# Three empty 32-byte pieces in the on-chip memory map of a decoder layer

## The reference

```python
x = x + attention(layernorm(x))        # 32 query heads, 8 key/value heads of 128; keys and values:
                                       # 16 cache blocks of 32 tokens picked by block_idx, and the 128 new ones
x = x + cross_attention(layernorm(x), ctx_4096, mask)   # 32 heads of 128, rmsnorm with ln_weight, position bias
x = x + (gelu(layernorm(x) @ W1 + b1) @ W2 + b2)        # 512 -> 2048 -> 512, NaN in y set to 0
```

## Time and profile before

| | |
|---|---|
| median of 3 runs | 2126.07 us (2125.66 to 2126.80) |
| the profiled execution's own time | 2129.9 us |
| its span, first to last instruction | 2128.0 us |
| TensorE matmul busy (PE) | 2076.8 us, 98% |
| TensorE weight load busy (PEld, beside PE) | 1789.8 us, 84% |
| VectorE busy (DVE) | 1500.9 us, 71% |
| ScalarE busy (ACT) | 1017.3 us, 48% |
| GpSimd busy (POOL) | 548.7 us, 26% |
| granted TensorE clock, mean | 0.991 of full speed |
| DMA | 76.90 MB, mean 36 GB/s; busy in the first 45 us |

### The profile page before, as it was taken

The page is one execution under the profiler, slowest core; times in us unless marked ns, Lnnn a source line. Parts: engine busy times, 40 slices in busy tenths (PEclk is TensorE's granted clock), DMA queues, the critical chain, the costliest instruction groups (busy, mean ns, idle before and its releaser), DMA issues.

```text
span 2128.0 us, 33928 instructions
## 1 busy us (share of the span) xinstructions
PE 2076.8 (98%) x11620; PEld 1789.8 (84%) x11620; DVE 1500.9 (71%) x2365; ACT 1017.3 (48%) x2232; POOL 548.7 (26%) x428
## 2 busy tenths in 40 slices
PE   8999999999999999999899999999999999999996
PEld 7888888888888888888788888888888888877885
DVE  6777777777777777777766666666666666677776
ACT  3555555555555555555544444444444444433331
POOL 2222122212221222221222222222222222214223
PEclk9999999999999999999999999999999999999998
DMA  8000000000000000011011111111111111010111
GB/s 234 16 21 16 15 20 20 16 14 20 20 20 10 20 20 20 13 47 40 31 59 43 42 42 37 38 39 38 42 42 42 42 42 42 23 35 25 49 44 50
DMA packets 44162, 76.90 MB, mean 36 GB/s; under 512 B 7378, under 2 KB 13650, under 8 KB 43602
## 3 DMA queue, kind: packets, MB, share of 16 engines
q1 hardware_dynamic: 43826, 74.15, 11.6%
q10 hardware_dynamic: 288, 2.10, 0.3%
HBM read 74.13 MB, written 2.10 MB: 36 GB/s over the span
## 4 chain that ended last, share of the span: by engine, by line
PE 88%; DVE 6%; issue 3%; ACT 2%; DMA 1%; SPq 0%; DVEq 0%; ACTq 0%
PE bank L1087 22%; PE bank L1089 22%; PE bank L1088 22%; PE bank L1156 9%; PE bank L1202 6%; PE bank L1355 1%; PE bank L1354 1%; PE bank L1270 1%; PE bank L1271 1%; PE bank L1329 1%; DVE negmax L872 1%; DVE V_lo L866 1%; DVE xn L802 1%; DVE pT_lo L910 1%; DVE q_lo L904 1%
## 5 line engine op out<-in xcount | busy, mean ns | idle before, releaser
L882 DVE SCALAR_TENSOR_TENSOR xacc<-bank,rinv,xacc 128x512 f32<-128x512 f32 x512 | 375.7, 745 | 71.2 <-PE bank L1089 71.1
L481 ACT ACTIVATE pT_hi<-bank 128x512 fp32r<-128x512 f32 x320 | 190.8, 597 | 202.3 <-PE bank L1202 202.0
L872 DVE TENSOR_REDUCE negmax<-bank 128x1 f32<-128x640 f32 x256 | 210.2, 821 | 36.9 <-PE bank L1156 29.6
L535 ACT ACTIVATE prob<-bank,negmax 128x640 f32<-128x640 f32 x256 | 202.6, 791 | 66.2 <-DVE negmax L872 66.2
L910 DVE TENSOR_TENSOR pT_lo<-bank,pT_hi 128x512 fp32r<-128x512 f32 x320 | 217.5, 680 | 2.4 <-ACT pT_hi L481 2.4
L1202 PE MATMUL bank<-ident,prob 128*128 128x128 f32 x1280 | 191.3, 272 | 0.0
L1202 PEld LDWEIGHTS bank<-ident,prob 128*128 128x128 f32 x1280 | 159.2, 140 | 18.6
L378 POOL TENSOR_TENSOR wo_lo<-wo_raw,wo_hi 128x512 fp32r<-128x512 f32 x32 | 41.4, 1293 | 430.8 <-ACT wo_hi L481 430.8
L628 ACT ACTIVATE xprob<-xscore,negmax 128x128 f32<-128x128 f32 x256 | 99.5, 391 | 96.2 <-DVE negmax L963 96.2
L1087 PE MATMUL bank<-xwv_hi,cT_hi 128*128 128x256 f32 x512 | 143.4, 280 | 1.4 <-DVE xV_lo L930 1.4
L1088 PE MATMUL bank<-xwv_lo,cT_hi 128*128 128x256 f32 x512 | 143.1, 280 | 0.0
(11 more groups left out here) (171 smaller groups left out, 5920.3 us busy)
## 6 DMA issues: line engine op xcount, KB each, us to landing
wq_raw<-in_wq SPq DMA_DIRECT2D x32, 256.0 KB, 2.6
wo_raw<-in_wo SPq DMA_DIRECT2D x32, 256.0 KB, 2.6
xwv_raw<-in_xwv SPq DMA_DIRECT2D x16, 512.0 KB, 3.5
xwk_raw<-in_xwk SPq DMA_DIRECT2D x32, 256.0 KB, 3.5
xwq_raw<-in_xwq SPq DMA_DIRECT2D x32, 256.0 KB, 3.4
xwo_raw<-in_xwo SPq DMA_DIRECT2D x32, 256.0 KB, 2.6
w_raw<-in_w SPq DMA_DIRECT2D x32, 256.0 KB, 2.6
xacc<-in_x SPq DMA_DIRECT2D x8, 256.0 KB, 4.9
```

The lines of the kernel that those rows point to most:

```text
L481: return s.activation(dst, src, ACT.Copy)
L535: s.activation(prob[:, slot, i, :].rearrange("p (a t) -> p a t", a=2), S_bank[i % 2], ACT.Exp, bias=negmax[:, slot, i:i + 1], scale=1.0, a ...
L872: v.tensor_reduce(negmax[:, slot, i:i + 1], S_bank[i % 2], mybir.AxisListType.XY, ALU.max, negate=True).then_inc(a["max"], 1)
L882: v.scalar_tensor_tensor(xacc[:, 4 * half + i, :], M, rinv[:, k, i:i + 1], xacc[:, 4 * half + i, :], ALU.mult, ALU.add).then_inc(sems["y"], 1)
```

## The change

Three tensors of 8 float32 per partition (32 bytes) are allocated and never used. The instructions are the same on every engine and in the same order, word for word but for the source line numbers, which are 1 to 3 higher in the changed file. Only addresses differ.

```diff
@@ -56,6 +56,7 @@
         negmax = sb(ctx, "negmax", [P, 2, 4])
         rowsum = sb(ctx, "rowsum", [P, 2, 4])
         rinv = sb(ctx, "rinv", [P, 2, 4])
+        sb(ctx, "shift2", [P, 8])
...
@@ -107,6 +108,7 @@
             xwo_raw = sb(ph, "xwo_raw", [P, 2, D])
             xwo_hi, xwo_lo = pair(ph, "xwo", [P, 2, D])
             anykey = sb(ph, "anykey", [P, B])
+            sb(ph, "shift3", [P, 8])
             comb = sb(ph, "comb", [P, 2, 4, P])
...
@@ -127,6 +129,7 @@
             w2_raw = sb(ph, "w2_raw", [P, 2, D])
             w2_hi, w2_lo = pair(ph, "w2", [P, 2, D])
             b1_sb = sb(ph, "b1_sb", [P, 2])
+            sb(ph, "shift4", [P, 8])
             b2_sb = sb(ph, "b2_sb", [P, D])
```

## The result

The changed kernel takes 2117.19 us in the median of 6 runs (2114.55 to 2120.43), the kernel before 2126.3 (2125.66 to 2127.58, 6 runs): a ratio of 0.9958, interval 0.9945 to 0.9971. It is faster by 9 us. That lies in the predicted range (2113 to 2133), but the forecast was "no change within 0.2%", and this is 0.4%. By the prediction's own signs of being wrong, the time left 2122 to 2130, and a group of 1536 matmuls, the values, moved its pace by 3.8%. The profiled execution took 2116.57 us, its span 2114.6, against 2129.9 and 2128.0.

A forecast was written before the change was run, and what follows sets the result against it. The prediction took TensorE, busy 2076.8 of 2128.0 us, as the bound, with load waits in the first 50 us. Its five terms (TensorE, VectorE, ScalarE, GpSimd, loads) were each 0, giving 2126 us, range 2113 to 2133.

The forecast's parts named there:

- no change within 0.2%: Whole kernel: the median stays at 2126 us, within the 4.3 us a measurement can tell; chance 0.60.
- signs of being wrong: Whole kernel: wrong if any group of 768 matmuls moves its pace by 3% or the time leaves 2122 to 2130.
- The frame: Whole kernel: no instruction, transfer or wait changes; TensorE's matmul pace passes to the end nearly one to one.
- VectorE, ScalarE and GpSimd cost nothing: Engines beside TensorE: cost 0 on the path, with VectorE bounded at 0.1 us and ScalarE under 1.5 us.
- (a): TensorE: unlike starts of stream and weights cost a pause; 3072 matmuls gain 20.5 us, to 2106, or half, 2116; chance 0.12.
- (c): Head: K and V cache block loads were slow because of the start; `wv` lands 6.9 us earlier, 2119; chance 0.04.
- (d): Changed distances between tensors make accesses collide differently: 1 to 2 groups of 768 move, 5 to 10 us either way; chance 0.10.
- the first term: TensorE matmuls: cost 0, with bounds per matmul of 6.7 ns gain and 6.7 (keys) or 3 ns (values) loss.
- the difference in pace at most: TensorE, 256 columns: `xwv` over `cT` at 280 ns against `xpT` over `xV` at 283 bounds the pace difference to 3 ns.
- (b): TensorE: start 32 was the fast one; keys lose 5.1 us (2131), with values 9.7 us together (2136); chance 0.14.

The follow-up runs named there:

- m1: Separate kernel, layer not computed, TensorE alone: blocks of equal matmuls over pairs of start addresses, weights changed with every matmul; 1011.03 us.
- m2: Separate kernel, layer not computed, TensorE alone: 256-column blocks over pairs of starts, weights changed every third matmul, some pairs re-entered from short blocks; 1029.94 us.
- x9: Changed kernel with everything behind `xT` and `ident` another 64 bytes further on; 2120.27 us, ratio 0.9959 to the kernel before.
- x10: Changed kernel with one more 32-byte piece in front, all tensors 32 past a multiple of 64, distances kept; 2118.46 us, ratio 0.995 to the kernel before.
- x7: The change with its first piece alone, against the changed kernel: `comb`, `xq`, `hid` and the like back at 32; 2124.02 us, ratio 0.9978 to the kernel before.
- x3: Changed kernel with `xwk`, `xwq`, `xwo`, `w1`, `w2` and small tensors between at 32 past a multiple of 64; 2123.23 us, ratio 0.9976 to the kernel before.

## Why the prediction was right or wrong

The frame held. The change touches no instruction, the gain came through TensorE's pace alone and passed nearly one to one to the end in cross attention. In attention, whose stretch looked just as full, it did not. VectorE, ScalarE and GpSimd cost nothing: `q_lo` 692 ns after 691, `xwq_hi` 622 after 623, `w_lo` 1291 after 1287. That the range held the time is partly luck: its lower part was there for (a), (c) and half of (d), and only (d), with 0.10, comes near what happened.

The step that failed is the first term, "*TensorE* ... I take 0, because the majority of 512-column kinds run at 233 ns with starts of both sorts". It had two faults.

* It sorted pairs by each tensor's start modulo 64. What m1, m2 and the kernels show is the distance of the two, modulo 256, and then the entry. By distances the rows of before fall into line with m1: queries at 96 (233 ns), V product at 64 (233), keys at 0 (227). The change took the queries from 96 to 64 (2805 to 2762 in attention), and left values and keys where they were. A majority over kinds that differ in this says nothing.
* It took the values' 280 ns against 283 of another shape of use as "the difference in pace at most", so as a bound. A recorded duration (280 ns) is more than twice the distance between two starts (118), and what the 256-column matmuls could win was not in the sum at all. The gain was 4.4 ns on the 1440 matmuls of the loop's 60 groups: 6.3 us, more than any other term. The start times of a group, which the trace of before had, would have shown 2826 for 24.

The rivals. (a), unlike starts cost a pause, had the right sign and forecast queries at 0.68 us for three; attention's came to 0.69 (2762 / 4), cross attention's to 0.69 and 0.70 in turn, and the full 20.5 us were far off. Like starts aren't its cause either: in the changed kernel half of the cross queries stay at 2799. It noted that VectorE or ScalarE may take over. In attention 2.2 us of queries left the loop at -0.1, but that one of these took over isn't shown, and x9 speaks against a hard limit, since there the loop kept 2.5 of 3.7 us. (b), 32 is the fast start, is refuted: keys 2751 after 2760, values faster. (c), the cache blocks' loads, would have shown over 300 GB/s where the earlier trace rows has 245 and the kernel after 262, and the head won 1.6 us, not 6.9: refuted, but for a part of that; x10, with every start at 32, reaches its first score at 51.33 us, sooner than the changed kernel's 51.62. (d), interplay by the distances between tensors, was nearest in mechanism and in size (5 to 10 us), and got a chance of 0.10. It named the distance to `xT`, which fits attention's queries (2805 ns at 96, 2762 at 64, 2736 at 0 in x9) but leaves open why m1 has one pace at 96 and 64 and why cross queries at 64 run at 2760 and 2799 in turn; that the values would change pace with their own distance unchanged, through the matmuls ahead of them, nobody had listed.

The chance of 0.60 for "no change" was too high for what the rows showed: groups of equal shape already differed by 3% with no reason found, and a change that moves nearly every tensor can redraw them. The nine further kernels that only move tensors lie between 0.995 and 1.0011.

The Trainium skill (SBUF — State Buffer, Who interferes with whom) gives TensorE two independent read ports, one for the streamed operand and one for weights, and says of it that it never waits on anyone. The runs agree that no other engine is needed for the pauses (m1 and m2 have none running); they disagree on the independence, since the pace of one stream changes with where the weights lie (m2: stream at 64, 117.8 ns over weights at 0, 120.0 over 64).

What stays open: why a series settles at one pace or another, which entries lead to the fast one (the distance in `c_out` alone doesn't: x7 shares the kernel before's, 224, and has slow values, 1396 and 1395 ns per 6 in `c_out`, but x3 shares it too, with values at 2720), and what took back the queries' gain in attention. A layout with queries at distance 0 as in x9 and all values at 2720 might beat both kernels by a few us more; it was not tried.

## What to carry to other kernels

Where TensorE is the bound, read its pace from start times, group by group, and compare it with the best pace that any group of that shape shows, or TensorE alone in a short kernel like m2: a group at 118 instead of 113 ns is a gain lying in the memory map. What decided here was the pair of operands, mostly by their distance modulo 256 bytes, and what ran before, not the alignment of either; so after any edit that moves tensors or puts a matmul between others, expect some tenths of a per cent (nine layouts here: -0.5 to +0.1), and test a few empty pieces against each other instead of trusting a rule. A forecast of "no change" for such an edit needs all groups to be at one pace first.

## What the runs showed of the hardware that was not expected

* For fp32r matmuls at 2.4 GHz whose weights change every matmul or every third, 256 columns take 113.3 to 120.0 ns in most blocks (up to 123.3 in m1), 512 columns 227 to 234, by the two operands' start addresses and by what ran before them; no other engine needs to run.
* The pace is periodic in the distance with 256 bytes as far as tried (weights at 0 and the stream at 0, 256, 512: 120.0 each; weights at 64 and the stream at 0, 256, 512: 113.5, 113.5, 113.3).
* Once settled, a series kept its pace to the end of its block of 96 matmuls in m2 and 144 in m1, and the same pair can have two or three (m2), 4% apart.
* For 512 columns the best distance was 0 (227 ns in m1); for 256 columns 0 was among the worst (120.0 in m2), and 112 and 192 were the best (113.3), though 112 gave 120.0 with weights at 48 in m1, and 16 and 64 reached 113.3 too after some entries.
